# A graph layer on one core: eight consecutive edges per partition row, summed on VectorE by their two destinations, two scatter products per 1024 edges instead of eight, and gathers written out without a loop

## The chip, the cores and the metric

The kernel runs on one core of one Trainium2 chip. The metric is the device time of one execution in microseconds (us). The kernel before takes 2069.61 us, the median of 3 runs (2066.08 to 2070.26). The engines are called by the profile's names: PE is TensorE, PEld its weight loads, DVE is VectorE, ACT is ScalarE, POOL is GpSimd, SP is the engine that issues most plain DMAs. PSUM is the memory that PE writes to, SBUF the working memory; both have 128 partitions.

## The reference

There are 6250 nodes with 128 features and 206250 edges, sorted by destination, each with a source node and 50 edge features. A destination has 33 edges on average. Cut to what matters, it computes:

```python
h = relu(layernorm(x))
W = silu(edge_attr @ fw1 + fb1) @ fw2 + fb2      # per edge, 50 -> 128 -> 128
t = silu(h @ aw1 + ab1) @ aw2 + ab2              # per node
msg = W * t[src]                                 # gather by source, product per edge
agg = segment_sum(msg, dst)                      # sum by destination
out = x + h + silu(agg @ ow1 + ob1) @ ow2 + ob2  # per node
```

Everything is float32.

## The kernel before

**Stages.** First the node stage: x is loaded, normalized, sent through the node MLP in 7 chunks of 7 tiles of 128 nodes, and the table t is written to DRAM (`node_table`). Then the edge stage: 1612 tiles of 128 edges, worked in 403 groups of 4 tiles (512 edges). 390 groups are "main" groups; their rows of t are gathered from the table. 13 groups are "early" groups: their x rows were gathered during the node stage (52 gathers, `e_x`), and the node MLP is run on them inside the edge stage. The output MLP of the nodes (`output`) is put between the edge groups, as soon as the destinations of a stretch of nodes are complete.

**One main group.** POOL gathers 4 x 128 rows of 512 bytes with 4 indirect DMAs (L272), each of 128 indices, one per partition. PE multiplies the edge features (50 x 512) with fw1 (L685), ACT applies silu (L344), PE multiplies with fw2, 4 products of 128 edges (L692), and adds the bias by one bf16 product (L694). The result lies in PSUM with one edge per partition. DVE multiplies it with the gathered rows (L554): 128x512, `msg`. Edge number p of a tile is in partition p, so the sum over destinations is a product over the partitions: DVE builds a one-hot matrix of each edge's destination within a window of 64 nodes (L537, 128x256 for 4 tiles, two SBUF inputs: `iota` and `rel`), PE multiplies `msg` with it, 4 products of 128x64 that add up in PSUM (L702), and DVE adds the 64 columns to `agg` at the group's first destination (L546; the offset is loaded from SBUF into a register by L542). `agg` holds the features in the partitions and the nodes in the columns. A float32 product is two matmul instructions in the trace.

**Order.** Each engine runs its own program, written out by hand; semaphores tie them. A turn is 13 groups in a loop (`turn`), and each group of a turn has its own place in `xg`, the buffer for gathered rows. POOL waits for `msg_done` of the same place one turn earlier, so it can be up to 13 groups, 52 gathers, ahead. The indices come in two halves, `src_a` and `src_b`, which SP loads again each turn. PE's order in a turn is: hidden of group i+1, filters of group i, window of group i-1. 5 legs (`LEGS`) each have 5 turns, 2 early groups and an output of 7 tiles; 2 turns with an early group each and 3 turns with an output each follow.

**A way out.** Before the edge stage DVE and PE count the edges that do not fit the windows or come out of order. With the inputs at hand the count is zero, and the slow loop at the end (`edges_left`) is not entered.

Of the kernel before, what the change touches and what calls it, by code (L numbers as in the profile page):

```python
# [5 lines left out]
P = 128  # L20
F = 128
NG = 50
N_NODES = 6250
N_EDGES = 206250
NODE_TILES = -(-N_NODES // P)
CH = 7
# [5 lines left out]
EDGE_TILES = -(-N_EDGES // GC) * TPG  # L32
GROUPS = EDGE_TILES // TPG
SLOTS = 13
TT = SLOTS * TPG
TURNS = GROUPS // SLOTS - 1
EARLY = TURNS * TT
SLOTS_A = 7
PARTS = ((0, SLOTS_A), (SLOTS_A, SLOTS))
WIN = 64  # L40
RW = 512
R_WINDOWS = -(-(N_NODES + 1) // RW)
AGG = max(R_WINDOWS * RW, N_NODES + WIN)
EPS = 1e-5
assert NODE_TILES == N_CHUNKS * CH and GROUPS == (TURNS + 1) * SLOTS
# [3 lines left out]
LEGS, LEG_TURNS, LEG_EARLY = N_CHUNKS - 2, 5, 2  # L49
LEG_GROUPS = LEG_TURNS * SLOTS + LEG_EARLY  # L50
REST_TURNS = SLOTS - 1 - LEGS * LEG_EARLY
LAST_TURNS = TURNS - LEGS * LEG_TURNS - REST_TURNS
LAST_OUT = 4
REST_OUT = NODE_TILES - LEGS * CH - LAST_TURNS * LAST_OUT
assert REST_TURNS > 0 and LAST_TURNS > 0 and 0 < REST_OUT <= CH
OUTPUTS = LEGS + 1 + LAST_TURNS

CHECKPOINTS = [((c + 1) * LEG_TURNS * TT, (c + 1) * CHC) for c in range(LEGS)] + \
    [((TURNS - LAST_TURNS + t) * TT, (LEGS * CH + REST_OUT + t * LAST_OUT) * P) for t in range(LAST_TURNS)]


def main_part(eng, turn, early, output):

    early(0, 0, 1, 0, N_CHUNKS)
    with eng.Fori(0, LEGS) as leg:
        with eng.Fori(0, LEG_TURNS) as t:
            turn(leg * LEG_GROUPS + (t * SLOTS + 1), leg * LEG_TURNS + t)
        mlp = leg * (LEG_EARLY + 1) + (N_CHUNKS + 1)  # L70
        early(leg * LEG_GROUPS + (LEG_TURNS * SLOTS + 1), leg * LEG_EARLY + 1, LEG_EARLY, leg + 1, mlp)
        output(leg * LEG_GROUPS + (LEG_GROUPS + 1), leg * CH, CH, leg, mlp + LEG_EARLY)
    at, mlp = LEGS * LEG_GROUPS + 1, N_CHUNKS + 1 + LEGS * (LEG_EARLY + 1)
    with eng.Fori(0, REST_TURNS) as t:
        turn(t * (SLOTS + 1) + at, t + LEGS * LEG_TURNS)
        early(t * (SLOTS + 1) + (at + SLOTS), t + (LEGS * LEG_EARLY + 1), 1, t + (LEGS + 1), t + mlp)
    at += REST_TURNS * (SLOTS + 1)
    mlp += REST_TURNS
    output(at, LEGS * CH, REST_OUT, LEGS, mlp)
    with eng.Fori(0, LAST_TURNS) as t:  # L80
        turn(t * SLOTS + at, t + (TURNS - LAST_TURNS))
        output(t * SLOTS + (at + SLOTS), t * LAST_OUT + (LEGS * CH + REST_OUT), LAST_OUT, t + (LEGS + 1),
               t + (mlp + 1))

RING3 = [s % 2 for s in range(SLOTS - 1)] + [2]
RING2 = [s % 2 for s in range(SLOTS)]


def back(ring, s):

    return next(d for d in range(1, SLOTS + 1) if ring[(s - d) % SLOTS] == ring[s])


def done(place, s=0, d=0):


    return place + (SLOTS + 1 + s - d)  # L100


def run(c, d=0):

    return c + (3 - d)


def gnn_layer(nc, x, src_t, dst_t, attr_t, fw1, fb1, fw2, fb2, aw1, ab1, aw2, ab2, ow1, ob1, ow2, ob2, out):
# [8 lines left out]
    with ExitStack() as ctx:  # L117
# [18 lines left out]

        xs = sb("xs", [P, NODE_TILES, F])
# [4 lines left out]
        stats = sb("stats", [P, TT, 6])  # L142
        moments = sb("moments", [P, 4, NODE_TILES])

        dst_i = sb("dst_i", [P, EDGE_TILES], i32)
        first_dst = sb("first_dst", [1, GROUPS])
        rel = sb("rel", [P, EDGE_TILES])
        cover = sb("cover", [P, EDGE_TILES], bf16)
        in_order = sb("in_order", [P, EDGE_TILES], bf16)
        n_well = sb("n_well", [P, 1])  # L150
        n_left = sb("n_left", [P, 1], i32)
# [660 lines left out]
```

## Time and profile before

| | |
|---|---|
| runs, median | 2069.61 us (2066.08 to 2070.26, 3 runs) |
| profiled execution, its span and its own time | 2768.5 us |
| instructions | 27356 |
| PE busy | 2047.6 us (74%) |
| POOL busy | 1538.0 us (56%) |
| DVE busy | 607.5 us (22%) |
| ACT busy | 344.5 us (12%) |
| mean granted TensorE clock | 0.673 of 2.4 GHz |
| DMA | 159.11 MB, mean 57 GB/s |

The page gives no time of the profiled execution other than its span, so the two are the same number here. It is 1.34 times the median of the runs. The profiled execution and the others thus differ by 699 us, and a row of the trace that holds a wait has to be read with that in mind; a row that holds the duration of an instruction less so.

How to read it: busy time is the time in which an engine had an instruction in work. The idle time before an instruction is put down to what released it; "issue" means that the profile shows nothing that was waited for, "remote" or "another core or an unknown queue" that the releaser could not be found. The granted clock is a number between 0 and 1; 0.50 is TensorE at 1.2 GHz and 1.00 TensorE at 2.4 GHz.

### The profile page before, as it was taken

The page shows a single profiled execution, that of the slowest core. Times are in us where ns is not written, and L with a number is a line of the kernel's source. Part 1 is how long each engine was busy: PE and PEld are TensorE (multiplying, and loading weights), DVE is VectorE, ACT ScalarE, POOL GpSimd, SP SyncE. Part 2 cuts the span into 40 slices and gives each one's busy share as a digit, 9 for nine tenths or more (in the row PEclk, how much of TensorE's full clock was granted, in tenths as well). Part 3 has the DMA queues.
Part 4 walks back from the last instruction along what each step waited for, and adds up shares of the span by engine and source line. Part 5 has one row for each costly group of instructions (what it writes and reads, how often), then busy time and mean ns, then how long its engine had stood idle before and what let it go on. Part 6 is the DMA issues. An engine that isn't in the chain of part 4 may idle for free.

```text
span 2768.5 us, 27356 instructions
## 1 busy us (share of the span) xinstructions
PE 2047.6 (74%) x8016; PEld 1446.7 (52%) x8144; DVE 607.5 (22%) x1429; ACT 344.5 (12%) x542; POOL 1538.0 (56%) x1619
## 2 busy tenths in 40 slices
PE   1447778777777877777868777787787777888678
PEld 1234555555555555545645555564555555555455
DVE  2611212222121222212212211222121222222112
ACT  1211011110111111101111111011011111111001
POOL 7365665546565555655555666644566554555560
PEclk8657766666666766666576666656566665666677
DMA  4312222222222222222212212211222221121220
GB/s 115 86 42 61 64 54 61 54 54 63 50 62 57 55 58 57 60 60 51 60 50 60 61 51 63 62 47 48 59 63 62 51 59 47 50 60 49 56 64 13
DMA packets 85742, 159.11 MB, mean 57 GB/s; under 512 B 36260, under 2 KB 56150, under 8 KB 82720
## 3 DMA queue, kind: packets, MB, share of 16 engines
q0 software_dynamic: 51584, 105.75, 14.8%
q1 hardware_dynamic: 26568, 49.57, 7.3%
q10 hardware_dynamic: 7568, 3.54, 0.5%
q8 instruction: 9, 0.15, 0.0%
q14 instruction: 13, 0.11, 0.0%
HBM read 152.32 MB, written 6.42 MB: 57 GB/s over the span
## 4 chain that ended last, share of the span: by engine, by line
PE 47%; another core or an unknown queue 36%; issue 8%; DVE 5%; ACT 1%; DVEq 1%; SPq 0%; DMA 0%; ACTq 0%
PE banks L692 14%; PE banks L685 14%; PE banks L702 13%; PE banks L694 3%; DVE msg L554 2%; PE banks L637 2%; DVEq L542 1%; PE banks L632 1%; ACT hid L344 1%; PE banks L732 1%; DVE agg L546 0%; ACT mid L318 0%; DVE stats L521 0%; SPq L210 0%
## 5 line engine op out<-in xcount | busy, mean ns | idle before, releaser
L272 POOL DMA_INDIRECT xg<-node_table,src_a x840 | 802.5, 955 | 675.7 <-DVE msg L554 383.3
L272 POOL DMA_INDIRECT xg<-node_table,src_b x720 | 684.2, 950 | 476.1 <-issue 209.4
L692 PEld LDWEIGHTS banks<-fw_s,hid 128*128 128x128 f32 x3224 | 590.8, 274 | 631.3 <-issue 393.5
L702 PE MATMUL banks<-onehot,msg 128*128 128x64 f32 x3224 | 583.7, 345 | 350.7 <-DVE msg L554 257.8
L692 PE MATMUL banks<-fw_s,hid 128*128 128x128 f32 x3224 | 688.0, 380 | 207.1 <-ACT hid L344 166.5
L702 PEld LDWEIGHTS banks<-onehot,msg 128*128 128x128 f32 x3224 | 604.2, 267 | 403.4 <-issue 371.6
L685 PE MATMUL banks<-attr,fw_s 50*128 50x512 f32 x780 | 624.0, 899 | 16.4 <-DVE res L587 15.6
L554 DVE TENSOR_TENSOR msg<-banks,xg 128x512 f32<-128x512 f32 x390 | 269.2, 690 | 1299.9 <-remote 723.8
L344 ACT ACTIVATE hid<-banks,cols 128x512 f32<-128x512 f32 x403 | 275.4, 687 | 2176.2 <-PE banks L685 1086.0
L546 DVE TENSOR_TENSOR agg<-agg,banks 128x64 f32 x403 | 89.5, 222 | 610.5 <-remote 289.6
L685 PEld LDWEIGHTS banks<-attr,fw_s 50*128 50x128 f32 x780 | 160.6, 250 | 92.1 <-issue 62.6
L537 DVE TENSOR_TENSOR onehot<-iota,rel 128x256 f32<-128x256 f32 x403 | 171.3, 425 | 14.5 <-issue 14.5
L694 PE MATMUL banks<-fb_rows,ones_b 128*128 128x512 bf16 x275 | 146.0, 531 | 0.0
L259 POOL DMA_INDIRECT e_x<-in_x,e_src x52 | 50.1, 964 | 17.2 <-issue 15.5
L637 PE MATMUL banks<-aw_s,mid 128*128 128x128 f32 x202 | 31.3, 310 | 34.2 <-ACT mid L318 24.6
L694 PEld LDWEIGHTS banks<-fb_rows,ones_b 128*128 128x128 bf16 x403 | 52.9, 131 | 0.0
L637 PEld LDWEIGHTS banks<-aw_s,mid 128*128 128x128 f32 x202 | 29.6, 223 | 36.3 <-ACT mid L318 26.4
L626 PE MATMUL banks<-ident,hs 128*128 128x128 f32 x101 | 20.0, 343 | 33.9 <-issue 33.9
L318 ACT ACTIVATE mid<-banks,cols 128x512 f32<-128x512 f32 (+2 forms) x29 | 23.5, 812 | 165.5 <-PE banks L632 75.9
L626 PEld LDWEIGHTS banks<-ident,hs 128*128 128x128 f32 x101 | 14.4, 174 | 53.0 <-issue 52.5
L732 PE MATMUL banks<-hT,aw_s 128*128 128x512 f32 x26 | 22.3, 952 | 24.6 <-DVE hT L562 21.8
L637 PEld LDWEIGHTS banks<-ow_s,mid 128*128 128x128 f32 x98 | 16.1, 253 | 18.3 <-issue 11.3
(76 smaller groups left out, 264.2 us busy)
## 6 DMA issues: line engine op xcount, KB each, us to landing
attr<-in_attr SPq DMA_DIRECT2D x30, 700.0 KB
attr<-in_attr SPq DMA_DIRECT2D x30, 600.0 KB
xg<-node_table,src_a POOLq DMA_INDIRECT x840
xg<-node_table,src_b POOLq DMA_INDIRECT x720
xs<-in_x SPq DMA_DIRECT2D x7, 448.0 KB, 4.5
node_table<-res SPq DMA_DIRECT2D x7, 448.0 KB, 3.0
out<-res ACTq DMA_DIRECT2D x5, 448.0 KB
e_attr<-in_attr SPq DMA_DIRECT2D x13, 100.0 KB
```

What stands on the lines that cost most here:

```text
L259: pool.indirect_dma_start(e_x[:, j, :], None, x[:, :], bass.IndirectOffsetOnAxis(ap=e_src[:, j:j + 1], axis=0)).then_inc(gathered[j // TPG ...
L272: pool.indirect_dma_start(xg[:, s, j * P:(j + 1) * P], None, table[:, :], bass.IndirectOffsetOnAxis(ap=src_ab[k][:, col:col + 1], axis=0))\
L344: act.activation(hid[:, b, :], hid_ps[b], ACT.Silu, bias=cols[:, 0:1]).then_inc(hid_done, 1)
L537: dve.tensor_tensor(onehot[:, b, :, :], iota[:, 0:WIN].rearrange("p (o k) -> p o k", o=1).to_broadcast([P, TPG, WIN]), r.to_broadcast([P, ...
L546: dve.tensor_tensor(window, window, sum_ps[k][:, 0:WIN], ALU.add).then_inc(win_added, 1)
L554: dve.tensor_tensor(msg[:, b, :], fil_ps[b], xg[:, s, :], ALU.mult).then_inc(msg_done, 1)
L637: i = pe.matmul(to[:, j * P:(j + 1) * P], mid[:, j * P:(j + 1) * P], weights, start=True, stop=True)
L685: pe.matmul(hid_ps[b], w["fw1_s"][:, :], features, start=True, stop=True).then_inc(hid_sum, 1)
L692: pe.matmul(fil_ps[b][:, j * P:(j + 1) * P], hid[:, b, j * P:(j + 1) * P], w["fw2_s"][:, :], start=(j == 0), stop=False)
L694: pe.matmul(fil_ps[b], ones_b[:, :], fb2_rows[:, :, :].rearrange("p j f -> p (j f)"), start=False, stop=True).then_inc(fil_done, 1)
L702: i = pe.matmul(sum_ps[k][:, 0:WIN], msg[:, b, j * P:(j + 1) * P], onehot[:, b, j, :], start=(j == 0), stop=(j == TPG - 1))
L732: pe.matmul(e_l1_ps, w["aw1_s"][:, :], hT[:, 0:GC], start=True, stop=True).then_inc(s_l1, 1)
```

## The change

Edges are laid out anew on the host: of each 1024 edges (a "pair" of half groups), partition p holds edges 8p to 8p+7, so that a partition row holds 8 consecutive edges. Since the edges are sorted by destination, such a row has at most two destinations with these inputs; 21% of the rows have two. There are 202 pairs (1616 tiles): 196 main pairs with 1568 gathers, and 6 early pairs with 48. A turn is 4 pairs, and `xg` holds 4 pairs, 32 gathers, where it held 52.

For each pair DVE writes both halves of `msg` (two instructions of 128x512 as before), then `mask` writes a second copy of it, 128x1024, multiplied with `other` (1 where an edge's destination is not the row's first), and `row_sums` adds the 8 edges of a row, for the copy and for the original: 128x2048 values in, 128x256 out. Of the one-hot matrices there are two per pair, each 128x64: that of the row's first destination, and that of its last less that of its first. PE multiplies the two row sums with them: two products per pair instead of eight.

POOL's gathers are written out one after the other with constant waits; all of `src` is loaded once, by one DMA in the node stage. POOL's first table gather also waits for `s_cover` to reach 3, that is, until DVE has made `same`, `same_last` and `low` out of the destinations. The tests for the way out are made per row of 8 edges and per pair; the count is zero here as well. SP loads the edge features by halves of two pairs (400 KB, where it was 700 and 600 KB).

```diff
-SLOTS = 13
-TT = SLOTS * TPG
+L = 2 * TPG
+PAIR_EDGES = L * P
+PAIRS = -(-N_EDGES // PAIR_EDGES)
+EDGE_TILES = PAIRS * L
+SLOTS = 4
+EARLY_PAIRS = 6
+MAIN_PAIRS = PAIRS - EARLY_PAIRS
...
-            def turn(place, n):
-                for s in range(SLOTS):
-                    k = s // SLOTS_A
-                    if s in (0, SLOTS_A):
-                        pool.wait_ge(src_in[k], n * 16 + 16)
-                    pool.wait_ge(msg_done, done(place, s, SLOTS))
-                    pool.sem_inc(slot_taken, 1)
-                    for j in range(TPG):
-                        col = (s - k * SLOTS_A) * TPG + j
-                        pool.indirect_dma_start(xg[:, s, j * P:(j + 1) * P], None, table[:, :],
-                                                bass.IndirectOffsetOnAxis(ap=src_ab[k][:, col:col + 1], axis=0))\
-                            .then_inc(gathered[s], 16)
+            pool.wait_ge(src_in, 16)
+            pool.wait_ge(s_cover, 3)
             pool.wait_ge(s_tab, 16 * run(N_CHUNKS - 1))
+            for q in range(MAIN_PAIRS):
+                for h in range(2):
+                    if q >= SLOTS:
+                        pool.wait_ge(msg_done, run(2 * (q - SLOTS) + h))
+                    for j in range(TPG * h, TPG * h + TPG):
+                        pool.indirect_dma_start(xg[:, q % SLOTS, j, :], None, table[:, :],
+                                                bass.IndirectOffsetOnAxis(ap=src[:, q * L + j:q * L + j + 1], axis=0))\
+                            .then_inc(gathered[q % SLOTS][h], 16)
...
-                dve.tensor_tensor(onehot[:, b, :, :],
-                                  iota[:, 0:WIN].rearrange("p (o k) -> p o k", o=1).to_broadcast([P, TPG, WIN]),
-                                  r.to_broadcast([P, TPG, WIN]), ALU.is_equal)
+            def one_hot_first(b, q, signal):
+                dve.tensor_tensor(onehot[:, b, 0, :], iota[:, 0:WIN],
+                                  ends[:, 0, bass.ds(q, 1)].to_broadcast([P, WIN]), ALU.is_equal).then_inc(signal, 1)
+
+            def one_hot_last(b, q, signal):
+                dve.scalar_tensor_tensor(out=onehot[:, b, 1, :], in0=iota[:, 0:WIN], scalar=ends[:, 1, bass.ds(q, 1)],
+                                         in1=onehot[:, b, 0, :], op0=ALU.is_equal, op1=ALU.subtract).then_inc(signal, 1)
+
+            def mask(b, q, signal):
+                dve.tensor_tensor(msg[:, b, 1, :, :], msg[:, b, 0, :, :],
+                                  other[:, bass.ds(q * L, L)].rearrange("p (j o) -> p j o", o=1).to_broadcast([P, L, F]),
+                                  ALU.mult).then_inc(signal, 1)
+
+            def row_sums(b, signal):
+                dve.reduce_sum(sums[:, b, :, :], msg[:, b, :, :, :].rearrange("p m j f -> p m f j"),
+                               AX.X).then_inc(signal, 1)
...
+                    dve.wait_ge(msg_done, run(2 * q + 1))
+                    mask(b, q, masked)
+                    dve.wait_ge(masked, q + 1)
+                    row_sums(b, red_done)
...
-                for j in range(TPG):
-                    i = pe.matmul(sum_ps[k][:, 0:WIN], msg[:, b, j * P:(j + 1) * P], onehot[:, b, j, :],
-                                  start=(j == 0), stop=(j == TPG - 1))
-                i.then_inc(win_done, 1)
+            def window_of(b, signal):
+                for m in range(2):
+                    i = pe.matmul(sum_ps[b][:, 0:WIN], sums[:, b, m, :], onehot[:, b, m, :], start=(m == 0), stop=(m == 1))
+                i.then_inc(signal, 1)
```

How the order of DVE changes, inside a turn, first before, for one group of 4 tiles (`banks` is PSUM, `xg` the gathered rows):

```order
L537 TENSOR_TENSOR onehot<-iota,rel 128x256
L553 REGISTER_ALU
L554 TENSOR_TENSOR msg<-banks,xg 128x512
L542 REGISTER_ALU
L542 TENSOR_LOAD dst_i
L542 ISA x2
L546 ISA
L546 TENSOR_TENSOR agg<-agg,banks 128x64
```

And DVE inside a turn after the change, for the first pair of a turn, which is two such groups (the window of the pair before is added between the second product and the mask from the second pair on):

```order
L535 TENSOR_TENSOR onehot<-iota,ends 128x64
L567 ISA
L568 ISA
L569 TENSOR_TENSOR msg<-banks,xg 128x512
L539 ISA
L539 SCALAR_TENSOR_TENSOR onehot<-iota,ends,onehot 128x64
L568 REGISTER_ALU
L569 TENSOR_TENSOR msg<-banks,xg 128x512
L543 ISA
L543 TENSOR_TENSOR msg<-msg,other 128x1024
L548 TENSOR_REDUCE sums<-msg 128x256
```

Two large one-hot instructions have become two small ones, and an instruction with two SBUF inputs of 1024 elements and a reduction stand behind each second product, ahead of the next pair's first.

PE inside a turn before, for one group (L685 hidden, L692 and L694 filters, L702 window):

```order
L685 MATMUL banks<-attr,fw_s 128x512
L690 REGISTER_ALU
L692 MATMUL banks<-fw_s,hid 128x128 x4
L694 MATMUL banks<-fb_rows,ones_b 128x512
L699 REGISTER_ALU
L702 MATMUL banks<-onehot,msg 128x64 x4
```

PE inside a turn after, for one pair (L709 hidden, L713 and L715 filters, L720 window):

```order
L709 MATMUL banks<-attr,fw_s 128x512
L732 REGISTER_ALU
L713 MATMUL banks<-fw_s,hid 128x128 x4
L715 MATMUL banks<-fb_rows,ones_b 128x512
L709 MATMUL banks<-attr,fw_s 128x512
L732 REGISTER_ALU
L713 MATMUL banks<-fw_s,hid 128x128 x4
L715 MATMUL banks<-fb_rows,ones_b 128x512
L737 REGISTER_ALU
L739 REGISTER_ALU
L720 MATMUL banks<-onehot,sums 128x64 x2
```

The window products come once in a pair, and they are 2 where they were 8; hidden and filters stand as they stood.

## Rows read from the trace of the kernel before

**Rows 1.** Page: busy time of each engine, and the chain that ended last.

```profile
PE 2047.6 (74%) x8016; PEld 1446.7 (52%) x8144; DVE 607.5 (22%) x1429; ACT 344.5 (12%) x542; POOL 1538.0 (56%) x1619
...
PE 47%; another core or an unknown queue 36%; issue 8%; DVE 5%; ACT 1%; DVEq 1%; SPq 0%; DMA 0%; ACTq 0%
```

**Rows 2.** Groups by line, POOL's table gathers: busy us, mean ns | idle before.

```profile
L272 POOL DMA_INDIRECT xg<-node_table,src_a x840 | 802.5, 955 | 675.7 <-DVE msg L554 383.3 <-issue 292.4
...
L272 POOL DMA_INDIRECT xg<-node_table,src_b x720 | 684.2, 950 | 476.1 <-issue 209.4 <-DVE msg L554 197.6 <-DVE msg L577 69.1
```

**Rows 3.** Timeline, first and last table gather: start, us, instruction, idle before.

```profile
106.70 5.61 DVE L475 MEMSET agg<- 128x6656 f32 x1 [1.34 <-issue]
...
110.47 3.07 POOL L272 DMA_INDIRECT xg<-node_table,src_a  x1 [41.12 <-issue]
...
2706.80 0.94 POOL L272 DMA_INDIRECT xg<-node_table,src_b  x1 [0.30 <-issue]
```

**Rows 4.** Windows of 3 us, all engines, then clock, DMA share and GB/s.

```profile
core 0: us, PE busy (x) PEld busy (x) DVE busy (x) ACT busy (x) POOL busy (x), PEclk, DMA share, GB/s
...
634.00:637.00 3.00, 3.00 (x14) 2.02 (x14) 0.22 (x1) 0.02 (x1) 0.94 (x1) 0.79 0.15 44
...
652.00:655.00 3.00, 0.07 (x1) 0.00 (x0) 0.00 (x0) 0.00 (x0) 2.25 (x3) 0.56 0.16 44
```

**Rows 5.** The chain from 620 to 650 us: start, us, what.

```profile
622.68 1.60 PE banks L702 x8
624.28 2.00 PE banks L685 x2
...
630.32 2.00 PE banks L685 x2
...
642.28 1.05 PE banks L685 x2
...
644.64 0.84 PE banks L702 x8
645.48 1.05 PE banks L685 x2
```

**Rows 6.** Timeline, POOL and DVE near 1462 us: a gather beside L583.

```profile
1461.65 0.94 POOL L272 DMA_INDIRECT xg<-node_table,src_b  x1 [0.30 <-issue]
1462.90 1.65 POOL L272 DMA_INDIRECT xg<-node_table,src_b  x1 [0.30 <-issue]
1464.86 0.94 POOL L272 DMA_INDIRECT xg<-node_table,src_b  x1 [0.30 <-issue]
...
1462.64 1.09 DVE L583 TENSOR_TENSOR xs<-xs,rows 128x896 f32 x1
```

**Rows 7.** Timeline, gathers beside a one-hot and beside a reduction.

```profile
571.67 0.43 DVE L537 TENSOR_TENSOR onehot<-iota,rel 128x256 f32<-128x256 f32 x1
...
571.77 1.14 POOL L272 DMA_INDIRECT xg<-node_table,src_b  x1 [0.30 <-issue]
...
122.48 1.83 DVE L512 TENSOR_REDUCE n_well<-in_order 128x1 f32<-128x1612 bf16 x1
...
123.79 0.94 POOL L272 DMA_INDIRECT xg<-node_table,src_a  x1 [0.30 <-issue]
```

**Rows 8.** Gather at 619.78 us, and the DMA share in quarters of a us.

```profile
619.78 0.94 POOL L272 DMA_INDIRECT xg<-node_table,src_a  x1 [10.68 <-DVE msg L554]
...
621.50:621.75 0.25, 0.25 (x1) 0.50 0.56 148
621.75:622.00 0.25, 0.22 (x1) 0.50 0.02 0
```

**Rows 9.** Timeline of the first early group, PE and DVE.

```profile
147.25 1.05 PE L637 MATMUL banks<-aw_s,mid 128*128 128x128 f32 x8
...
178.33 0.69 DVE L572 TENSOR_TENSOR e_row<-banks,rows 128x512 f32<-128x512 f32 x1 [34.72 <-remote]
```

**Rows 10.** Timeline, DVE around the early groups and output of leg one.

```profile
586.16 0.22 DVE L546 TENSOR_TENSOR agg<-agg,banks 128x64 f32 x1 [1.49 <-PE banks L702]
...
611.33 1.09 DVE L587 TENSOR_TENSOR res<-banks,xs 128x896 f32<-128x896 f32 x1 [5.54 <-PE banks L637]
...
618.29 0.69 DVE L554 TENSOR_TENSOR msg<-banks,xg 128x512 f32<-128x512 f32 x1 [5.47 <-PE banks L694]
```

**Rows 11.** Gathers by source line: ns min/median/max, first and last start.

```profile
L272 POOL DMA_INDIRECT xg<-node_table,src_a x840: 938/944/3067, 110.5 to 2669.3; - x168
```

More of the change, by code:

```diff
@@ L62, in main_part, with last_starts @@
+assert LEGS * LEG_TURNS + sum(n for n, _ in LAST) == TURNS
+def last_starts():
+    turn, tile = LEGS * LEG_TURNS, LEGS * CH + REST_OUT
+    for turns, tiles in LAST:
+        yield turn, turns, tile, tiles
+        turn, tile = turn + turns, tile + tiles
+CHECKPOINTS = [((c + 1) * LEG_TURNS * SLOTS, (c + 1) * CHC) for c in range(LEGS - 1)] + \
+    [(turn * SLOTS, tile * P) for turn, _, tile, _ in last_starts()]
 def main_part(eng, turn, early, output):
-    early(0, 0, 1, 0, N_CHUNKS)
+    early(0, N_CHUNKS)
@@ L77, in main_part @@
[L77 to L94, printed above, removed]
@@ L97, in done @@
-def done(place, s=0, d=0):
-    return place + (SLOTS + 1 + s - d)
+            turn(leg * LEG_TURNS + t)
+        early(leg + 1, leg * 3 + (N_CHUNKS + 2))
+        output(leg * CH, CH, leg, leg * (LEG_TURNS * SLOTS) + LEG_TURNS * SLOTS, leg + 2, leg * 3 + (N_CHUNKS + 4))
+    mlp = N_CHUNKS + 2 + 3 * LEGS
+    output(LEGS * CH, REST_OUT, LEGS, LEGS * LEG_TURNS * SLOTS, EARLY_PAIRS, mlp)
+    for k, (first_turn, turns, first, tiles) in enumerate(last_starts()):
+        with eng.Fori(0, turns) as t:
+            turn(t + first_turn)
+        output(first, tiles, LEGS + 1 + k, (first_turn + turns) * SLOTS, EARLY_PAIRS, mlp + 1 + k)
@@ new lines, in gnn_layer @@
+        dst_i = spare[:, 0:EDGE_TILES].bitcast(i32)
+        same, same_last = (spare[:, EDGE_TILES + i * (EDGE_TILES // 2):EDGE_TILES + (i + 1) * (EDGE_TILES // 2)].bitcast(bf16)
+                           for i in range(2))
+        low, high, least, fit = (spare[:, 2 * EDGE_TILES + i * PAIRS:2 * EDGE_TILES + (i + 1) * PAIRS] for i in range(4))
+        r_src = sb("r_src", [P, 1], i32)
+        r_x = xg[:, 0, 0, :]
+        r_all = xg[:, 1:, :, :].rearrange("p s j f -> p (s j f)")
+        r_dst = r_all[:, 0:EDGE_TILES]
@@ L580, in output @@
-            def output(place, first, n, before, mlp):
+            def one_hot_first(b, q, signal):
[4 more added lines that the diff above has]
+                                         in1=onehot[:, b, 0, :], op0=ALU.is_equal, op1=ALU.subtract).then_inc(signal, 1)
@@ L582, in output @@
+            def output(first, n, k, pairs, earlies, mlp):
                 xc = xs[:, bass.ds(first, n), :]
@@ L734, in early @@
-            def early(place, n, count, before, mlp):
-                early_start(place, n, 0, before)
-                early_layer1(n, mlp)
-                for r in range(count):
-                    filters(place, r, 2, 1)
-                    if r + 1 < count:
-                        early_start(place, n, r + 1, before)
-                    pe.wait_ge(s_mid, run(mlp + r))
-                    pe.wait_ge(s_res, run(mlp + r, 1))
-                    layer2(e_l2_ps, TPG, w["aw2_s"][:, :], s_l2)
-                    if r + 1 < count:
-                        early_layer1(n + (r + 1), mlp + (r + 1))
-                    window(place, r, 2, 0, 1)
@@ L748, in output @@
[L748 to L749 removed]
+                pe.matmul(to, ones_b[:, :], fb2_rows[:, :, :].rearrange("p j f -> p (j f)"), start=False,
+                          stop=True).then_inc(signal, 1)
+            def window_of(b, signal):
+                for m in range(2):
+                    i = pe.matmul(sum_ps[b][:, 0:WIN], sums[:, b, m, :], onehot[:, b, m, :], start=(m == 0), stop=(m == 1))
+                i.then_inc(signal, 1)
@@ L750, in output @@
+            def output(first, n, k, pairs, earlies, mlp):
+                pe.wait_ge(win_added, pairs + AHEAD)
+                pe.wait_ge(e_added, earlies)
                 pe.wait_ge(s_mid, run(mlp, 1))
```

520 lines of the change are left out of this document (279 added, 241 removed).

## The prediction

> **What bounds the kernel now.** I read the page's busy times and its chain first. The chain gives PE 47% and "another core or an unknown queue" 36% [rows 1]: taken alone, this is a kernel that PE paces, with many stalls. Then the medians: the profiled execution took 2768.5 us, the runs 2070 us. Something of 699 us stands in the trace and not in the runs, so I looked for the part that cannot shrink. That is POOL. The groups by line show 1560 table gathers that take 1486.7 us, with idle time ahead of them [rows 2]. A gather takes 0.94 us and the next begins 0.30 us after it, over and over [rows 6]: 1.247 us from start to start, also where no wait is between them. The reader should see in rows 3 that the first starts at 110.47 us. So POOL without any wait needs 110.5 + 1486.7 + 1559 x 0.30 (467.7) = 2064.9 us to the end of its last gather, and some 12 us are left behind it (landing 1, product 0.7, window 1, add 0.2, output MLP of 4 tiles about 6, write 3): 2077 us. That is the median of the runs within 0.3%. The same from the other side: the idle time of rows 2 is 1151.8 us, less 41.1 ahead of the first gather [rows 3] and 467.7 of steady gaps leaves 643 us of waits, most for `msg`; and the span ends 60.8 us after the last gather. Take out the 643 and 49 of the 61: 2077.
>
> Could PE be the pace of the runs and this sum a coincidence? From the chain a group takes PE 6.04 us at the low clock (two starts of L685 six us apart, 624.28 and 630.32) and 3.20 us at the high one (642.28 and 645.48) [rows 5]. The clock comes back to 1.00 in dense work and falls to 0.50 where PE is idle (0.79 in the slice from 634 us, dense; 0.56 from 652 us, where PE worked 0.07 of 3 us) [rows 4]. PE dense throughout would do 403 groups in 1290 us, so 2070 is not PE's own speed. I take the runs to be paced by POOL, with PE waiting for rows and changing between its clocks: 4.99 us per group is between 3.20 and 6.04, and 13 places in `xg` hide the turns of it.
>
> **The change part by part**, as what it does to POOL's column (a pair is 8 gathers, 9.98 us):
>
> Gathers. 1568 in place of 1560: +8 x 1.247 = +10. Writing them out saves nothing inside a group, where there was no wait before. The 52 unlooped gathers of x and the looped ones have the same 0.30 gap.
>
> PE. It loses 6 of 8 window products per pair. 4 products (x8) cost 0.84 at the high and 1.60 at the low clock [rows 5], so a pair falls from 6.40 to 5.14, or from 12.08 to 9.68 us. As POOL paces at 9.98, this gain is beside the path: 0.
>
> DVE. L583 shows 1.09 us for 896 elements, the one-hot 0.43 for 256 [rows 6, 7], so 0.16 fixed and 1.04 ns per element. The mask of 1024 takes 1.22 us. The reduction of 1612 elements took 1.83 [rows 7], so 2048 take 2.29. One pair on DVE: 2 x 0.69 + 1.22 + 2.29 + 0.22 + 2 x 0.22 and gaps of 0.5, about 6 us of 9.98; it was 2.7. DVE has the room. Behind the mask and reduction stands the next pair's first product, whose rows land 4 gathers (5 us) after the last pair's: mask, reduction and one-hot end about 4.6 us after that product began. So no wait from this.
>
> The mask and the gathers. This is the term that decides. A gather that starts while DVE has an instruction with two SBUF inputs in work is longer: at 1462.90 us L583 had 0.83 us to go and the gather took 1.65 in place of 0.94; at 571.77 a one-hot had 0.33 to go and it took 1.14 [rows 6, 7]. Both say: the delay is what DVE has left, less 0.13 us. Beside a reduction, one input, a gather took 0.94 [rows 7]. The mask has two SBUF inputs. At a random phase a mask of 1.22 delays by 1.09 x 1.09 / 2 / 1.247 = 0.48 us. The phase isn't random if POOL paces: rows land 2.0 us after their gather starts (619.78, traffic over in the slice from 621.75) [rows 8], the second product starts 0.15 later, the window add follows, and the mask runs from about 3.05 to 4.27 after that gather's start; the third gather behind it starts at 3.74 and waits 4.27 - 3.74 - 0.13 = 0.40. I take 0.43: 196 x 0.43 = +84. Bounds: 0 and 196 x 1.09 = 214, as a phase is kept for whole stretches. The old one-hots go: the gathers' busy sum is 1486.7 against 1560 x 0.944 = 1472.6 [rows 2, 11]; of these 14, 9 are theirs: -9. The new ones of 0.22 us add next to nothing.
>
> The Trainium skill, "SBUF — State Buffer", section "SBUF: two separate sides", has the pair of ports that VectorE and GpSimd share as an exclusive lock, held for the whole instruction by whoever came first. The half that delays the gather agrees with these rows. The other half would have the mask wait behind a gather, up to 0.94 us; that would be taken from DVE's spare 4 us and leave the sum as it is.
>
> Head. POOL's first gather now waits for `low`, behind a memset of `agg` of 5.3 us, two comparisons of 1616 elements (1.83 each, as the reduction of 1612) and four small ones: from 106.7 [rows 3] to about 117. Before, it started at 110.5 but took 3.07, held up itself: +4. Then `xg` is full after 32 gathers, at 157 us. The first early group was at L637 at 147.25 [rows 9]; its row came at 178.33 behind a wait of 34.72 that I don't count in the runs. The early pair, two groups one after the other with mask and reduction, would end near 159 and the first main product near 166: +9. Before, 52 places lasted to 175.
>
> Legs. Between the last window add of a leg and the next leg's first product 32 us pass (586.16 to 618.29) [rows 10]. Now it is 32 + 1.2 + 2.3, about 36, and POOL's lead is 32 gathers less the landing, some 36 us. It was 61. No loss on paper; I put 1 us for each of 5, +5, bounds 0 and 75 (five stalls of 15).
>
> Tail. Mask and reduction on the end +3.5, a fifth tile +0.5: +4.
>
> Sum on the profile's own numbers: 2077 + 10 - 9 + 84 + 4 + 9 + 5 + 4 = 2184. The column came out 7 above the median, so 2177 us, 5.2% slower.
>
> **The rivals.**
>
> A. PE paces the runs, and POOL's 1.247 us is stretched by profiling. For it: the chain [rows 1] and the 643 us for which POOL waited. Against it: two sums within 0.3%, a spread of the runs of 0.2% although the clock swings, and gathers that keep 0.94 + 0.30 also in the stalls. Then a pair gains 1.26 to 2.40 us; at the mean 9.3 us per pair of the runs, (2070 - 250) / 195, halfway: 196 x 1.8 = 350 at most, 1720 us. POOL's floor, lower than I think but not by much, stops it earlier: 1750 to 2060, middle 1930.
>
> B. The lock costs nothing here, as the mask falls between two gathers. It needs a landing 0.4 us sooner than rows 8 have it. Then 2177 - 84 = 2093, 1.1% slower; with the head and legs smaller too, 2070.
>
> C. The other side of A, worse than my forecast: stalls like those of the trace also occur in the runs, and 32 places do not cover them as 52 did. For each stall longer than about 36 us less PE's lag POOL stands still. Place: the legs and the three outputs. The trace's stall of 12 us at 649 us would be covered, one of 35 [rows 9] not. It decides from some 5 us per leg and output; at 15 us for 5 legs more than in my sum, 2177 + 70 = 2247.
>
> D. PE at the low clock is the bound. It waits more, so it has more idle holes, and the clock falls in these [rows 4]. A pair at the low clock takes 9.68, under 9.98, and with the mask's delay POOL needs 10.4. It decides only if PE loses over 0.7 us per pair; each 0.1 beyond that costs 20 us: about 2250. The Trainium skill, "TensorE: Matmul & The Clock Gate", section "HAM oscillation — how this bites in real kernels", warns of work that becomes thinner than its waits, since every stretch then starts cold. That speaks against thinning PE's work; here it would remove the high clock and change nothing until that margin is gone.
>
> E. The change does not do what it says: edges left over for the slow loop. With these inputs none is left, so no chance.
>
> **How the numbers follow.** My forecast 0.57, A 0.18, B 0.13, C and D together 0.12. Forecast 2177; its own range, with 0.15 to 0.8 us per mask, is 2120 to 2250. For 8 in 10 the range reaches down over B and the top of A, 2040 to 2255. A measurement of this kernel tells about 0.2%, 4 us, from no change. Faster is A, 0.18, and a part of B, 0.01; the same is 0.04, from B; slower is the rest, 0.77.
>
> **What would show it.** Right: in the changed trace gathers of 1.3 to 2.0 us about once in 8, each beside a mask, and the mean of a gather near 1.00 us; the reduction near 2.29 and mask near 1.22 us; the runs' time at POOL's sum of the new trace (first gather, busy, 0.30 gaps) plus about 15 us. Wrong: a run below 2060 us, which no POOL sum at 1.247 allows; gathers at 0.94 beside masks (B); a profiled span that fell by the window products while the runs did not, which would say that the profile's pace is not the runs'.

## The result and the profile after

The changed kernel takes 2389.74 us (median of 4 runs, 2383.77 to 2397.32) where the kernel before took 2068.61 us beside it: 1.155 times as long, 95% interval 1.1527 to 1.1576. The forecast was 2177 us, its range 2040 to 2255. The sign was right; of the 321 us that were lost it had a third.

The page of the changed kernel, busy times and the chain that ended last:

```profile
PE 1835.8 (77%) x5623; PEld 1104.8 (46%) x5727; DVE 1443.5 (60%) x1638; ACT 344.7 (14%) x538; POOL 1648.0 (69%) x1623
...
PE 61%; DVE 20%; issue 14%; DVEq 3%; DMA 1%; SPq 0%; ACT 0%; ACTq 0%
```

In the chain there is no POOL at all: it runs through PE and DVE in turn. In the kernel before, run again without the stalls of its first profile (e0 below), POOL heads the chain:

```profile
POOL 49%; PE 24%; issue 17%; DVE 4%; DMA 4%; POOLq 1%; SPq 1%; ACT 0%; DVEq 0%; ACTq 0%
```

PE is busy for 1835.8 us, 80 more than in e0 (1756.2), although it has some 2400 fewer matmul instructions to do (8144 in e0; 5727 here by the weight loads, of which 104 matmul records are missing). The groups by line (busy us, mean ns | idle before, with its releasers) give POOL's gathers, the reduction, the mask and the window products:

```profile
L267 POOL DMA_INDIRECT xg<-node_table,src x1568 | 1587.9, 1013 | 685.3 <-issue 468.0 <-DVE msg L569 217.3
...
L548 DVE TENSOR_REDUCE sums<-msg 128x256 f32<-128x2048 f32 x202 | 732.2, 3625 | 6.9
...
L543 DVE TENSOR_TENSOR msg<-msg,other 128x1024 f32<-128x1024 f32 x202 | 247.5, 1225 | 8.1 <-DVE msg L569 0.8
...
L720 PE MATMUL banks<-onehot,sums 128*128 128x64 f32 x808 | 180.1, 367 | 425.3 <-DVE sums L548 418.7 <-issue 5.9
```

The gathers are the answer to [rows 2]: 1013 ns in the mean where they took 950 to 955 (955 to 960 in e0), and 217.3 us of waits for `msg`. The view of waits (us in total, times, longest) shows that the window products wait 102 times for the row sums, 418.7 us in all:

```profile
PE banks L720 <- DVE sums L548: 418.7, 102, 6.8
...
POOL xg L267 <- DVE msg L569: 217.3, 33, 40.4
```

By the timeline 49 of the 102 waits stand at the ends of the 49 turns, 5.9 us each and 289 us together; 6 in the early pairs have 41 us, and the other 47 are of 2.5 us or less.

Against e0 (2064.9 us of span) the column of POOL closes to 0.1 us. "Idle" is the time ahead of a gather, steady gaps of 0.30 and waits; "end" runs from the start of the last gather to the end of the span.

| | first gather | gathers busy | idle | end | span |
|---|---|---|---|---|---|
| before, run again | 81.2 | 1493.8 | 475.4 | 15.6 | 2064.9 |
| after | 77.2 | 1587.9 | 685.3 | 46.4 | 2395.5 |
| difference | -4.0 | +94.1 | +209.9 | +30.8 | +330.6 |

The starts of POOL's waits in the timeline (start, us, instruction, idle before) name the places. There are five waits of 34 to 40 us (498, 870, 1244, 1617 and 1998 us), 181 us together, one per leg; the first of them:

```profile
498.49 0.94 POOL L267 DMA_INDIRECT xg<-node_table,src  x1 [36.41 <-DVE msg L569]
```

Four of the experiments below (e4, e7, e8, e9) were first run where the kernel before itself took 2724 us, and took 2672 to 2740 us there, which settles none of their questions, so the numbers below are those of their second runs (e4b and so on).

### The profile page after: what moved, and what is told of

It reads as the page before. It is cut to its first block, busy times and chain, and to the rows that moved or that the text cites. A ratio compares the mean times of both kernels' runs of the same rounds, so it can differ in the third digit from the quotient of the medians.

```text
span 2395.5 us, 21138 instructions
## 1 busy us (share of the span) xinstructions
PE 1835.8 (77%) x5623; PEld 1104.8 (46%) x5727; DVE 1443.5 (60%) x1638; ACT 344.7 (14%) x538; POOL 1648.0 (69%) x1623
## 4 chain that ended last, share of the span: by engine, by line
PE 61%; DVE 20%; issue 14%; DVEq 3%; DMA 1%; SPq 0%; ACT 0%; ACTq 0%
PE banks L709 26%; PE banks L713 22%; DVE sums L548 8%; DVE msg L543 6%; PE banks L720 5%; PE banks L715 3%; DVEq L552 2%; PE banks L665 1%; PE banks L660 1%; DVE msg L569 1%; PE banks L765 1%; DMA node_table<-res 1%; DVE onehot L535 1%; DVE agg L554 1%; PE banks L654 1%
## 5 line engine op out<-in xcount | busy, mean ns | idle before, releaser
L267 POOL DMA_INDIRECT xg<-node_table,src x1568 | 1587.9, 1013 | 685.3 <-issue 468.0
L713 PEld LDWEIGHTS banks<-fw_s,hid 128*128 128x128 f32 x3232 | 645.8, 294 | 482.5 <-issue 405.9
L709 PE MATMUL banks<-attr,fw_s 50*128 50x512 f32 x784 | 734.4, 1048 | 31.9 <-issue 17.5
L713 PE MATMUL banks<-fw_s,hid 128*128 128x128 f32 x3232 | 737.7, 400 | 1.0 <-issue 0.7
L548 DVE TENSOR_REDUCE sums<-msg 128x256 f32<-128x2048 f32 x202 | 732.2, 3625 | 6.9
L720 PE MATMUL banks<-onehot,sums 128*128 128x64 f32 x808 | 180.1, 367 | 425.3 <-DVE sums L548 418.7
L720 PEld LDWEIGHTS banks<-onehot,sums 128*128 128x128 f32 x808 | 174.5, 283 | 459.3 <-DVE sums L548 404.5
L709 PEld LDWEIGHTS banks<-attr,fw_s 50*128 50x128 f32 x784 | 192.3, 295 | 197.8 <-issue 182.5
L543 DVE TENSOR_TENSOR msg<-msg,other 128x1024 f32<-128x1024 f32 x202 | 247.5, 1225 | 8.1 <-DVE msg L569 0.8
L715 PE MATMUL banks<-fb_rows,ones_b 128*128 128x512 bf16 x300 | 166.6, 555 | 0.0
L254 POOL DMA_INDIRECT e_x<-in_x,src x48 | 58.9, 1226 | 16.0 <-issue 14.3
L715 PEld LDWEIGHTS banks<-fb_rows,ones_b 128*128 128x128 bf16 x404 | 55.5, 137 | 0.0
L539 DVE SCALAR_TENSOR_TENSOR onehot<-iota,ends,onehot 128x64 f32<-128x64 f32 x202 | 54.7, 271 | 0.0
L654 PEld LDWEIGHTS banks<-ident,hs 128*128 128x128 f32 x97 | 14.4, 179 | 47.1 <-issue 33.4
```

The source lines that it names most:

```text
L254: pool.indirect_dma_start(e_x[:, t, :], None, x[:, :], bass.IndirectOffsetOnAxis(ap=src[:, MAIN_TILES + t:MAIN_TILES + t + 1], axis=0))\
L267: pool.indirect_dma_start(xg[:, q % SLOTS, j, :], None, table[:, :], bass.IndirectOffsetOnAxis(ap=src[:, q * L + j:q * L + j + 1], axis=0))\
L543: dve.tensor_tensor(msg[:, b, 1, :, :], msg[:, b, 0, :, :], other[:, bass.ds(q * L, L)].rearrange("p (j o) -> p j o", o=1).to_broadcast([P ...
L548: dve.reduce_sum(sums[:, b, :, :], msg[:, b, :, :, :].rearrange("p m j f -> p m f j"), AX.X).then_inc(signal, 1)
L709: pe.matmul(to, w["fw1_s"][:, :], features, start=True, stop=True).then_inc(signal, 1)
L713: pe.matmul(to[:, j * P:(j + 1) * P], hid[:, b, j * P:(j + 1) * P], w["fw2_s"][:, :], start=(j == 0), stop=False)
```

## The experiments

In each table row the ratio is to runs of the kernel before on the same chip; these took 2073.42 us in the median beside e0 to e3, 2068.81 beside e4b, e7b, e8b and e9b, and 2072.23 beside e5 and e6. The sums of e2, e3, e4b and e6 are not the reference's, since these kernels leave out the real mask or add up the wrong neighbours; they serve to measure time. The others compute the whole reference. e0 is one run.

| kernel | us | ratio, 95% interval | gathers busy | idle | end |
|---|---|---|---|---|---|
| e0 before, again | 2066.73 | | 1493.8 | 475.4 | 15.6 |
| after | 2389.74 | 1.1552 (1.1527 to 1.1576) | 1587.9 | 685.3 | 46.4 |
| e1 pipelined | 2181.2 | 1.0533 (1.0505 to 1.0561) | 1545.9 | 532.8 | 22.0 |
| e2 mask's operand in PSUM | 2388.12 | 1.1522 (1.1464 to 1.158) | 1483.6 | 775.5 | 52.4 |
| e3 contiguous reduction | 2240.73 | 1.0795 (1.0764 to 1.0826) | 1576.1 | 554.8 | 36.7 |
| e4b e1 and e2 | 2109.13 | 1.0194 (1.0176 to 1.0211) | 1485.1 | 523.8 | 22.8 |
| e5 e1, msg by feature | 2171.03 | 1.049 (1.0453 to 1.0527) | 1547.7 | 521.4 | 20.6 |
| e6 e1, e2 and e3 | 2108.38 | 1.0174 (1.0157 to 1.0191) | 1487.2 | 522.9 | 20.6 |
| e7b before, 180 masks more | 2137.22 | 1.0333 (1.0316 to 1.035) | 1564.1 | 475.4 | 15.6 |
| e8b before, lead of 8 groups | 2074.94 | 1.0039 (1.0022 to 1.0055) | 1493.0 | 481.6 | 15.7 |
| e9b filler products | 2225.75 | 1.0761 (1.0743 to 1.0779) | 1590.1 | 530.2 | 21.2 |

**e0: the kernel before, once more.** No edit.

> The kernel before once more, for an execution whose profile takes as long as its runs (the first took 2768.5 us against 2069). Theory 1 (POOL's gathers pace it): first table gather near 77 us, gathers 1.247 us apart, few waits for msg, span 2060 to 2075. Rival (PE paces it): POOL waits over 100 us for msg with PE busy over 90%.

Its gathers by line:

```profile
L272 POOL DMA_INDIRECT xg<-node_table,src_a x840 | 802.5, 955 | 256.0 <-issue 252.3 <-DVE msg L554 2.7 <-DVE msg L577 0.9
L272 POOL DMA_INDIRECT xg<-node_table,src_b x720 | 691.3, 960 | 219.4 <-issue 215.8 <-DVE msg L554 3.7
```

In all 7.3 us of idle time stand to DVE's account, and no wait is longer than 0.5 us; the 643 us of waits of [rows 2] are gone. So POOL paces the kernel before, as the prediction read it. The first table gather starts at 81.20 (77 expected), not at 110.47 [rows 3], and PE is busy for 85%, with a mean clock of 0.779.

**e1: the last window of a turn behind the next turn's first pair.** PE's products and DVE's window add of the turn's last pair move into the next turn; only the first and last turn of a leg differ.

```diff
-            def turn(n):
+            def turn(n, first=False):
...
-                    if i % 2 == 1 and i > 1:
-                        window(i // 2 - 1)
-                window(SLOTS - 1)
+                    if i % 2 == 1 and (i > 1 or not first):
+                        window(n, i // 2 - 1)
```

> The changed kernel, with the last window product of a turn (and its add on DVE) moved behind the second group of the next turn, so that PE does not wait at each turn's end for mask and reduction. Theory 1 (that wait makes PE's turn, 43.4 us, as long as POOL's, 42.1, so it never catches up and each leg's early pair and output, 36 us, falls on POOL): the five stalls of 34 to 40 us shrink to under 10, 2390 falls by 150 to 210, to 2180 to 2240. Rival (32 places are too few to cover a leg, whatever PE does): stalls stay at 30 or more, 2350 to 2390. Rival (the longer gathers beside the mask are the bulk): 2380 or more.

Here is what it takes away. PE in the changed kernel around the end of a turn, in the timeline:

```profile
606.20 1.43 PE L713 MATMUL banks<-fw_s,hid 128*128 128x128 f32 x8
607.46 0.38 PE L715 MATMUL banks<-fb_rows,ones_b 128*128 128x512 bf16 x1
607.94 0.66 PE L720 MATMUL banks<-onehot,sums 128*128 128x64 f32 x4
614.51 1.11 PE L720 MATMUL banks<-onehot,sums 128*128 128x64 f32 x4 [5.91 <-DVE sums L548]
615.55 2.07 PE L709 MATMUL banks<-attr,fw_s 50*128 50x512 f32 x2
```

And DVE in the same stretch:

```profile
604.22 3.67 DVE L548 TENSOR_REDUCE sums<-msg 128x256 f32<-128x2048 f32 x1
...
607.98 0.68 DVE L569 TENSOR_TENSOR msg<-banks,xg 128x512 f32<-128x512 f32 x1
...
608.77 0.68 DVE L569 TENSOR_TENSOR msg<-banks,xg 128x512 f32<-128x512 f32 x1
...
609.60 1.22 DVE L543 TENSOR_TENSOR msg<-msg,other 128x1024 f32<-128x1024 f32 x1
610.86 3.59 DVE L548 TENSOR_REDUCE sums<-msg 128x256 f32<-128x2048 f32 x1
```

PE has its last filters done at 607.84 and, after the window of the pair before, only the last window left. DVE is still reducing the pair before until 607.9, so its two products of the last pair follow only then; it multiplies until 609.45, masks until 610.8, reduces until 614.45. PE stands for 5.91 us and then works at half speed: L709 x2 takes 2.07 us there. The windows of two whole turns of the changed kernel (from 571.5 and from 614.5 us):

```profile
core 0: us, PE busy (x) PEld busy (x) DVE busy (x) ACT busy (x) POOL busy (x), PEclk, DMA share, GB/s
571.50:614.50 43.00, 36.42 (x102) 21.61 (x103) 26.70 (x28) 5.50 (x8) 32.94 (x34) 0.54 0.27 69
614.50:658.00 43.50, 37.05 (x102) 22.52 (x104) 26.70 (x28) 5.50 (x8) 33.45 (x34) 0.54 0.27 69
```

The mean clock of each turn is 0.54, and a turn takes PE 43.5 us. The same view in finer windows, the first turn from 572 us on and the start of the next:

```profile
572.00:606.00 34.00, 33.42 (x86) 19.24 (x88) 18.28 (x21) 5.50 (x8) 26.14 (x26) 0.50 0.25 63
606.00:608.60 2.60, 2.50 (x14) 1.89 (x13) 2.60 (x4) 0.00 (x0) 1.99 (x3) 0.81 0.66 191
608.60:614.50 5.90, 0.00 (x0) 0.00 (x0) 5.82 (x6) 0.00 (x0) 4.38 (x6) 0.65 0.18 45
614.50:620.00 5.50, 5.49 (x11) 2.83 (x12) 0.45 (x2) 1.24 (x2) 4.28 (x5) 0.50 0.22 57
```

The clock is 0.50 from 572 to 606 us, although PE is busy for 33.4 of these 34 us, rises just before the hole, and is 0.50 again behind it. POOL's 32 gathers take 32 x 1.247 = 39.9 us and some 2 us for four masks, 42. PE is slower than that, so it never catches up, and `xg` is full for good. In e1 the waits of a leg's start fall to 5.6 to 16.1 us, 51 together (from 181; under 10 each were expected, and two are over), the end from 46.4 to 22.0, and the time by 209 us. The steady turns keep their low clock: 0.54 from 600 to 720 us of e1, as before (the mean of the whole run rises from 0.607 to 0.662), and PE no longer paces them. A part of the gain came unannounced: gathers' busy time fell by 42 us. DVE now waits for rows more than for PE, so the mask may lie otherwise among the gathers; no run tests this reason. The wait at the turn's end is the largest single cause.

**e2: the mask's second operand from PSUM.** The instruction has the same size, and only one SBUF input.

```diff
-                    mask(b, q, masked)
+                    other_mask(b, masked)
...
+                                  e_fil_ps.rearrange("p (o x) -> p o x", o=1).to_broadcast([P, 2, GC]),
```

> The changed kernel, with the mask's second operand read from PSUM (an old filter result in place of the 0/1 mask, so the sums are not the reference's), the same 1024 elements. Both theories: gathers beside it keep 0.94 us, the gathers' busy sum falls from 1588 to near 1485. Theory 1: PE's turn (43.4) is then longer than POOL's (40), so POOL only waits more: 2360 to 2390. Rival (the longer gathers are on the path): 100 us less, 2285.

Mask and reduction, and the gathers, by line:

```profile
L267 POOL DMA_INDIRECT xg<-node_table,src x1568 | 1483.6, 946 | 775.5 <-issue 439.4 <-DVE msg L575 336.1
...
L554 DVE TENSOR_REDUCE sums<-msg 128x256 f32<-128x2048 f32 x202 | 732.8, 3628 | 6.9
...
L548 DVE TENSOR_TENSOR msg<-msg,banks 128x1024 f32<-128x1024 f32 x196 | 238.1, 1215 | 1.7
```

The mask takes 1.22 us as before, but the gathers lose their excess: 1483.6 us, 0.946 each, 2 of 1568 longer than 1 us. So the delay comes from the second SBUF input. The time stays where it was, within 2 us: of the 104 us that the gathers lose, 90 come back as idle time of POOL and 6 at the end. Two turn starts in the timeline of POOL:

```profile
620.26 0.95 POOL L267 DMA_INDIRECT xg<-node_table,src  x1 [3.59 <-DVE msg L575]
...
663.69 0.95 POOL L267 DMA_INDIRECT xg<-node_table,src  x1 [3.62 <-DVE msg L575]
```

From turn to turn 43.4 us, of which POOL stands for 3.6: this is PE's turn seen from POOL. The mask's delay of the gathers cost the changed kernel nothing, since it lay inside another wait.

**e3: a contiguous reduction.** It sums 8 neighbouring values of `msg` instead of 8 that lie 128 apart.

```diff
-                dve.reduce_sum(sums[:, b, :, :], msg[:, b, :, :, :].rearrange("p m j f -> p m f j"),
+                dve.reduce_sum(sums[:, b, :, :],
+                               msg[:, b, :, :, :].rearrange("p m j f -> p m (j f)").rearrange("p m (x l) -> p m x l", l=L),
```

> The changed kernel, with the reduction reading its 2048 elements in the order in which they lie (8 neighbours are summed in place of 8 edges, so the sums are not the reference's). Expected for the instruction: 2.3 us where it took 3.63. Theory 1: the wait at a turn's end is 1.3 us shorter, 49 turns, up to 64 us and some of each leg's stall: 2310 to 2350. Rival (gathers and their lock alone pace it): no change, 2390.

```profile
L267 POOL DMA_INDIRECT xg<-node_table,src x1568 | 1576.1, 1005 | 554.8 <-issue 470.9 <-DVE msg L569 84.0
...
L548 DVE TENSOR_REDUCE sums<-msg 128x256 f32<-128x2048 f32 x202 | 461.7, 2286 | 7.0
```

2.29 us, the estimate of the prediction to the hundredth; strided it is 3.63. The time fell by 149 us to 2241, where 2310 to 2350 had been expected. 1.34 us less at the end of each turn are 49 x 1.34 = 66 us at most; the rest is a threshold. PE's turn was 43.5 us against POOL's 42, and 1.34 us less bring it to about POOL's own: in e3 no wait is left at a turn's start inside a leg. Between legs PE now gains a little on POOL, and the five waits are 18.8, 13.0, 13.0, 13.0 and 16.3 us, 74 together, where they were 181. These 107 us are most of the 149.

**e4b: e1 and e2 together.** Both edits.

> The same kernel as in e4 once more, since in that call the kernel before took 2724 us and not 2069, and everything ran at 2670 to 2740. Where the kernel before takes its 2069: theory 1, 2125 (POOL paces once PE has slack, and the longer gathers count then); rival, 2175 to 2185.

72 us below e1, or 67 if each is taken against the kernel before beside it (+40.3 and +107.8), with 1485.1 us of gathers against 1545.9; the forecast of 2125 was 16 too high. The same edit that gave nothing alone gives its full price once POOL paces: 67 / 196 = 0.34 us per mask, the excess of e1's gathers.

**e7b: the kernel before with the mask's kind of instruction.** 180 instructions of 128x1024 with two SBUF inputs that nobody waits for.

```diff
+                    if s % 2:
+                        dve.tensor_tensor(spare[:, :].rearrange("p (a b) -> p a b", b=RW),
+                                          iota[:, :].rearrange("p (o b) -> p o b", o=1).to_broadcast([P, 2, RW]), ...
```

> As e7, once more: where the kernel before takes 2069, 180 instructions with two SBUF inputs and 1024 elements each in the kernel before, 2145 at 0.43 us each, 2162 at 0.52; 2069 if it isn't the two inputs that hold the gathers.

```profile
L273 POOL DMA_INDIRECT xg<-node_table,src_a x840 | 831.4, 990 | 256.0 <-issue 251.1 <-DVE msg L555 3.7 <-DVE msg L583 1.2
L273 POOL DMA_INDIRECT xg<-node_table,src_b x720 | 732.7, 1018 | 219.4 <-issue 216.1 <-DVE msg L555 3.4
...
L557 DVE TENSOR_TENSOR spare<-iota,xs 128x1024 f32<-128x1024 f32 x180 | 218.6, 1215 | 0.0
```

68 us more, 0.38 us for each, all of it in the gathers' durations (+70.3 us) and none in the idle time. The prediction's 0.43 was a fair price for this mechanism, 8 us too much over 180 masks.

**e8b: the kernel before with a lead of 8 groups, not 13.**

```diff
-                    pool.wait_ge(msg_done, done(place, s, SLOTS))
+                    pool.wait_ge(msg_done, done(place, s, 8))
```

> As e8, once more: the kernel before with POOL at most 8 groups ahead. Theory 1: 2067 to 2085. Rival, the short ring by itself makes the stalls: 2240.

6 us. The shorter ring alone does little harm, in a kernel that has caught up with its gathers by the end of a leg.

**e9b: more work for PE.** 16 bf16 products of 128x512 into a bank that nobody reads, ahead of the last window of each turn of the changed kernel.

```diff
+                for _ in range(16):
+                    pe.matmul(e_fil_ps, ones_b[:, :], fb2_rows[:, :, :].rearrange("p j f -> p (j f)"), start=True, stop=True)
                 window(SLOTS - 1)
```

> As e9, once more: 16 bf16 products where PE is idle at the end of each turn. Clock as a part of the cause: 2250 or less, granted clock up from 0.61. Length of the hole only: 2390 to 2440.

The same place of a turn, PE in the timeline:

```profile
604.38 0.66 PE L720 MATMUL banks<-onehot,sums 128*128 128x64 f32 x4 [2.46 <-DVE sums L548]
604.88 5.30 PE L750 MATMUL banks<-fb_rows,ones_b 128*128 128x512 bf16 x16
610.97 0.66 PE L720 MATMUL banks<-onehot,sums 128*128 128x64 f32 x4 [0.79 <-DVE sums L548]
611.61 1.98 PE L709 MATMUL banks<-attr,fw_s 50*128 50x512 f32 x4
613.58 1.16 PE L713 MATMUL banks<-fw_s,hid 128*128 128x128 f32 x8
614.58 0.38 PE L715 MATMUL banks<-fb_rows,ones_b 128*128 128x512 bf16 x1
614.89 1.12 PE L709 MATMUL banks<-attr,fw_s 50*128 50x512 f32 x2
615.94 0.38 PE L713 MATMUL banks<-fw_s,hid 128*128 128x128 f32 x1
```

The filler fills the hole, the granted clock of the whole run rises from 0.607 to 0.733, L709 x2 takes 1.12 us where it took 2.07, and the kernel becomes 164 us faster by doing more. The last window still has to wait for the reduction (0.79 us behind the filler), so the 164 us don't come from a shorter wait: they come from the clock behind it, 1.00 from 611 to 620 us where the changed kernel has 0.50 from 614.5 to 620, and from the lead that a faster PE gives back (the leg waits are 4.7 to 16.8 us). e1 takes the wait away and leaves the steady turns at 0.54, e9b leaves the window where it was and raises the clock; each alone makes PE's turn short enough, so their 209 and 164 us do not add up. The Trainium skill, "TensorE: Matmul & The Clock Gate", section "HAM oscillation — how this bites in real kernels", describes a loop whose every wait sends the next stretch of products back to the low clock; the trace agrees (0.50 behind each hole, 1.00 behind the filler).

**e5 and e6: what is left.** e5 is e1 with `msg` laid out by feature, so that the reduction is contiguous and the 128x512 products write strided. e6 is e1, e2 and e3 together. The diff is of e5, and so are the two lines by group below.

```diff
+            def by_feature(b, m):
+                return msg[:, b, m, :, :].rearrange("p j f -> p (j f)").rearrange("p (x l) -> p x l", l=L)
```

> Pipelined turns, and msg laid out by feature, so that the reduction reads its 8 edges side by side; the products write strided in exchange. Computes the whole reference. Theory (POOL paces once PE no longer waits at turn ends; what is left beside the mask's delay is the leg waits): the reduction takes about 2.29 us in place of 3.63, the waits of POOL fall from 56 to about 35 us and the time from 2181 to about 2155 us. If the strided writes make a product longer than 0.69 us by as much as the reduction gains (0.67 us each of two), nothing changes: 2175 to 2190. Rival (DVE's own 9 us per pair paces somewhere): more than 40 us below 2181.

> Pipelined turns, the reduction reads contiguously and the mask takes its second operand from PSUM; sums are not the reference's. All three suspected costs are gone. Theory: only POOL's column is left, 77.6 to the first gather + 1482 busy + 1567 x 0.30 + a tail of about 20 = 2050, and leg waits of 20 to 40 us: 2075 to 2095 us, about 1% slower than before. Rival (the change has a further cost that none of the three removes): 2100 us or more.

```profile
L555 DVE TENSOR_REDUCE sums<-msg 128x256 f32<-128x2048 f32 x202 | 461.7, 2286 | 7.0
L576 DVE TENSOR_TENSOR msg<-banks,xg 128x512 f32<-128x512 f32 x392 | 426.5, 1088 | 642.7 <-DMA xg<-node_table,src 487.4 <-PE banks L725 149.5
```

In e5 the strided write costs a product 0.40 us (1.09 against 0.68), two per pair; the reduction gives 1.34. DVE has 0.5 us less to do, and the time is 10 us lower, which the intervals of the two ratios (1.0505 to 1.0561, 1.0453 to 1.0527) do not tell from nothing; it had been expected at 2155, or at 2175 and more if nothing changed. e6 missed its expectation by 13 us, on the side of its rival, a further cost that none of the three edits removes. It is no faster than e4b: once POOL paces, the length of the reduction is worth nothing. Its column against e0: first gather -3.4, busy -6.6, idle +47.5, end +5.0, together the 42.4 us by which the spans differ. The 47.5 are five waits at the legs of 6 to 11.5 us (43 together), one of 3.8 us where the ring is first full at 121 us, and 8 more gaps of 0.30; these overshoot by 2 us.

The traces show where the five waits come from. From the last product of a leg to the first of the next DVE takes 44.6 to 50.0 us in e6, and in each of the five legs POOL's wait is this stretch less 38 to 39 us, about what 32 gathers cover (32 x 1.247 = 39.9). In the kernel before the same stretch is 32.7 to 37.8 us (e0), so e8b, with the same 32 gathers of lead, has no wait over 1.4 us. It takes both, the longer stretch and the shorter ring: 52 gathers would cover 65 us. The longer stretch holds the early pair, two groups one after the other with mask and reduction behind them; which of its parts could be shortened was not tried.

No version here beats the kernel before; POOL's column alone, with no wait at all, would be 77.8 + 1487.2 + 1568 x 0.30 + 20.6 = 2056 us, 9 below the span of e0, and that needs e2's operand.

## Why the prediction was wrong, by its own steps

**What bounds the kernel before: right.** Cadence 0.94 + 0.30, POOL as the pace (e0). The sum of 2077 hit the median partly by luck: against the undisturbed trace the first gather was 29 us too late in it, and busy time, gaps and end were 7, 8 and 3 us too small.

**PE, "this gain is beside the path: 0": the step that failed,** together with DVE's "so no wait from this". I looked for a wait of the next pair's first product behind mask and reduction, and ruled it out because the rows land late. With the ring always full they do not: at 607.98 the product starts as the reduction ends, 1.6 us after its filters (606.4), and so do the products behind the other reductions inside the turn. There PE has other work and loses nothing. But I did not ask who waits for the end of the reduction. Inside a turn PE has hidden and filters of the next pair ahead of a window; at the turn's end it has nothing, and waits for product, mask and reduction, 5.9 us, 49 times. Without that wait (e1) the kernel is 209 of the 321 us faster. The order rows of the change show the window as the last thing in a pair, and the place at a turn's end was not drawn. Both kernels have this place; before, what stood between the last filters and the window was one product of 0.69 us.

**The clock: seen and mis-weighed.** Rival D had a pair at the low clock at 9.68 us against 10.4 of POOL, "decides only if PE loses over 0.7 us per pair". The trace has a turn of 43.5 us, 10.9 per pair, for POOL's 10.5: D is what happened. It lost 5.9 / 4 = 1.5 us per pair at the turn's end. PE thus lost 1.2 us per pair against 9.68, 0.5 beyond the margin, and D's price of 20 us for each 0.1 would have given some 2275. It was more, because with D the lead of POOL is gone too. The prediction's reading that the clock comes back in dense work [rows 4] did not hold here either: it was 0.50 for 34 us in which PE was busy for 33.4. D had 0.12 together with C.

**Legs, "no loss on paper", +5 with a bound of 75: measured +181.** The stretch between leg and leg was too short in the sum: from the last window add to the next product it is 38 to 45 us in the changed kernel, not 36. This alone is worth the 43 to 51 us of waits that e6 and e1 keep. The larger part is the lead of 36 us that was to cover it. A lead exists only if DVE and PE have caught up with the gathers by the leg's end. With PE's turn longer than POOL's they never do, so POOL pays nearly the whole stretch five times, 34 to 40 us. With a turn just shorter it pays 13 to 19 (e3), with a clear margin 6 to 16 (e1).

**Mask and lock: mechanism right, off the path.** Predicted 0.43 us per mask. The gathers' excess over 0.944 us is 107.7 us in the changed kernel, 0.55 per mask; 65.7 in e1, 0.34; in e7b the gathers take 70.3 us more than in e0, 0.39. The formula "what DVE has left, less 0.13 us" holds for the 193 gathers that start beside a mask in the changed kernel: 0.13 in the mean. The mask took 1.225 us (1.22 predicted). But e2 shows that it cost nothing in the changed kernel, and e4b that it cost 67 to 72 us in e1.

**The reduction: 3.63 us, not 2.29.** The row it was taken from reads contiguously [rows 7], the new one at a stride of 128 values. It is worth 149 us here (e3).

**Head and tail.** Predicted +4 and +9 for the head, measured -4.0 for the first gather and 5.7 us of wait at 122 us. The tail was +4 and is +30.8: with the ring always full the last gather, started at 2349.1 us, stands 27.7 us ahead of its product (2376.9).

Gathers (+10) and old one-hots (-9) were of the right size: 8 gathers more, and an excess of 21.2 us before (1493.8 - 1472.6) which e2 lacks.

Sum of the prediction +107; measured +330.6: legs 181 instead of 5, tail 31 instead of 4, other waits 20 instead of 0, gathers' busy time 94 instead of 83 (84 - 9 + 8), less a head that came out 11 us better.

## What to carry to other kernels

When work moves from one engine to another, walk each place where a loop turns over and ask what stands between the last independent work and the wait: a wait of 5.9 us there, which the steady state hides, cost this kernel 209 of the 321 us that it lost. Compare the turns of the engines, not only their busy times: with the second engine a few us shorter than the pacing one buffers cover most of a serial stretch, with it 1.5 us longer each is paid almost in full, and edits have prices that depend on which side one stands (the mask's operand: nothing in e2, 67 to 72 us in e4b; the contiguous reduction: 149 us in e3, nothing in e6). Take the duration of an instruction from a row with the same strides, not only with the same number of elements.

## What the runs showed of the hardware

- A reduction of 128x2048 float32 with 8 values per sum takes 3.63 us where these lie 128 values apart, 2.29 us where they are neighbours. A 128x512 product takes 0.69 us, and 1.09 us where it writes every eighth value.
- A gather that starts under a VectorE instruction with two SBUF inputs takes longer by what that instruction has left, less 0.13 us; with one input from PSUM it doesn't (188 gathers start beside a mask in e2, and take 0.95 us). The gather that started at 603.27 us shows it, beside the mask from 602.96:

```profile
602.96 1.23 DVE L543 TENSOR_TENSOR msg<-msg,other 128x1024 f32<-128x1024 f32 x1
603.27 1.73 POOL L267 DMA_INDIRECT xg<-node_table,src  x1 [0.30 <-issue]
...
605.30 0.94 POOL L267 DMA_INDIRECT xg<-node_table,src  x1 [0.30 <-issue]
```

  The reverse is not seen. Of the 202 masks of the changed kernel 118 start while a gather is under way; they take 1.23 us like the others, and the gap ahead of none of them is over 0.16 us. The Trainium skill, "SBUF — State Buffer", section "SBUF: two separate sides", would have VectorE wait behind a gather as well; this trace does not agree.
- PE became faster through added work: 16 products in the hole at a turn's end, and the kernel takes 164 us less (e9b).
- The granted clock can stay at 0.50 through dense work: from 572 to 606 us PE was busy for 33.4 of 34 us.
